# The rotary exchange of groups 4 to 7 moves from transfers into a second matmul, and the steps behind it move forward by one

## The reference

```
x = rmsnorm(tokens) * (1 + 0.1*tanh(scale)) + shift          # scale, shift from cond
q, k, v = split(x @ qkv_w.T + qkv_b)                         # 16 heads of 8 features
q, k = apply_rope(q), apply_rope(k)
#   rope: even' = even*cos - odd*sin ; odd' = even*sin + odd*cos
tokens = tokens + masked_attention(q, k, v) @ out_w.T + out_b      # SELF
query, src = rmsnorm(tokens), rmsnorm(side)
att = masked_attention(query @ wq.T, src @ wk.T, src @ wv.T) @ mha_out_w.T   # CROSS
gate = sigmoid([tokens, update] @ gate_w.T + gate_b); tokens += gate * update
h = rmsnorm(tokens); out = tokens + (silu(h @ g_w.T) * (h @ val_w.T)) @ down_w.T
```

## Time and profile before

| | |
|---|---|
| median of 3 runs | 519.72 us (514.06 to 522.11) |
| profiled execution | 517.94 us, its span 516.1 us |
| PE busy | 442.1 us (86%) |
| DVE busy | 350.1 us (68%) |
| ACT busy | 290.4 us (56%) |
| POOL busy | 190.8 us (37%) |
| mean granted TensorE clock | 0.937 |

### The profile page before, as it was taken

How to read it: one execution, slowest core, us unless ns; L and a number is a source line. 1 busy time by engine, 2 the same in 40 slices (tenths; PEclk the granted TensorE clock), 3 DMA queues, 4 the chain that set the end, 5 groups by cost and what they waited for, 6 DMA issues and landing times.

```text
span 516.1 us, 13226 instructions
## 1 busy us (share of the span) xinstructions
PE 442.1 (86%) x5219; PEld 308.3 (60%) x5219; DVE 350.1 (68%) x655; ACT 290.4 (56%) x644; POOL 190.8 (37%) x184
## 2 busy tenths in 40 slices
PE   3546889878897986999989988999999969999897
PEld 2115375756675664666577655866586748565664
DVE  2326655878885896698677866767748856856565
ACT  4321364577566664777576648486636744556243
POOL 4451140614433163528381828254542542000010
PEclk9975778899997999799999999999989999999999
DMA  3355442354353445344443443425140320000001
GB/s 77 87 174 174 131 122 88 100 162 151 100 162 107 140 121 153 103 128 121 131 137 108 117 140 97 153 67 163 43 149 25 98 92 3 23 3 22 22 1 42
DMA packets 62942, 52.04 MB, mean 101 GB/s; under 512 B 3803, under 2 KB 61728, under 8 KB 62880
## 3 DMA queue, kind: packets, MB, share of 16 engines
q1 hardware_dynamic: 60050, 49.07, 32.2%
q10 hardware_dynamic: 2830, 2.12, 1.4%
HBM read 8.55 MB, written 2.11 MB: 21 GB/s over the span
## 4 chain that ended last, share of the span: by engine, by line
PE 52%; DVE 11%; DMA 10%; ACT 8%; issue 8%; SPq 5%; POOL 4%; ACTq 1%; DVEq 0%; POOLq 0%
PE ps_o L403 8%; PE ps_a L366 7%; PE ps_g L320 7%; PE ps_b L386 6%; PE ps_g L461 5%; SPq L658 4%; DMA k_st<-part_k 4%; DVE top L1087 4%; PE ps_g L444 4%; PE ps_g L353 3%; DMA q_st<-top_t 3%; ACT probs L902 2%; DMA s_in<-in_fside_BxSxS 1%; ACT turned_in L838 1%; PE ps_g L418 1%
## 5 line engine op out<-in xcount | busy, mean ns | idle before, releaser
L1087 DVE TENSOR_REDUCE top<-ps_a 128x4 f32<-128x512 f32 x256 | 169.6, 680 | 106.1 <-PE ps_a L366 104.8
L902 ACT ACTIVATE probs<-ps_b 128x512 f32<-128x512 f32 x256 | 151.3, 595 | 143.6 <-PE ps_b L386 139.5
L366 PE MATMUL ps_a<-k_st,q_st 73*128 73x128 bf16 x1024 | 105.0, 228 | 27.8 <-DMA k_st<-part_k 15.0
L366 PEld LDWEIGHTS ps_a<-k_st,q_st 73*128 73x128 bf16 x1024 | 69.8, 101 | 79.5 <-issue 59.9
L386 PE MATMUL ps_b<-q_st,k_st 75*128 75x128 bf16 x1024 | 102.0, 223 | 9.4 <-ACT probs L902 7.5
L386 PEld LDWEIGHTS ps_b<-q_st,k_st 75*128 75x128 bf16 x1024 | 69.6, 99 | 18.5 <-issue 9.2
L403 PE MATMUL ps_o<-probs,v_pad 128*32 128x128 f32 x2048 | 73.3, 287 | 0.0
L403 PEld LDWEIGHTS ps_o<-probs,v_pad 128*32 128x32 f32 x2048 | 55.3, 115 | 24.1 <-issue 14.7
L728 POOL TENSOR_TENSOR f<-f 128x4 f32<-128x4 f32 x16 | 16.6, 1038 | 98.8 <-DVE f L1136 98.8
L320 PE MATMUL ps_g<-norm,w_t 128*128 128x512 f32 x66 | 37.1, 647 | 1.2 <-DVE hid L1178 1.2
L320 PE MATMUL ps_g<-turned_in,w_t 128*128 128x512 f32 x48 | 30.3, 717 | 5.0 <-ACT turned_in L838 4.8
(11 more groups left out here) (197 smaller groups left out, 677.6 us busy)
## 6 DMA issues: line engine op xcount, KB each, us to landing
q_st<-part_q SPq DMA_DIRECT2D x126, 128.0 KB
k_st<-part_k SPq DMA_DIRECT2D x120, 128.0 KB
x_in<-in_x SPq DMA_DIRECT2D x16, 256.0 KB, 4.5
q_st<-hid SPq DMA_DIRECT2D x18, 128.0 KB
s_in<-in_fside_BxSxS SPq DMA_DIRECT2D x8, 256.0 KB, 5.7
out<-t SPq DMA_DIRECT2D x8, 256.0 KB, 2.3
k_st<-hid SPq DMA_DIRECT2D x12, 128.0 KB
swap_q<-part_q SPq DMA_DIRECT2D x8, 128.0 KB, 2.3
```

The lines of the kernel that those rows point to most:

```text
L366: mm = pe.matmul(ps_a[q % 2][:, j * S:(j + 1) * S], st[0][i][0:R_MAX, h, b * S:(b + 1) * S], st[1][i][0:R_MAX, h, b * S:(b + 1) * S], star ...
L902: act.activation(probs[:, n % 2, q * T:(q + 1) * T], ps_b[q % 2][:, :], ACT.Exp, scale=SCALE).then_inc(exp_done, 1)
L1087: dve.tensor_reduce(top[:, n // 2 % 2, n % 2, QH * q:QH * (q + 1)], ps_a[q % 2][:, :].rearrange("p (h k) -> p h k", h=QH), AX.X, ALU.max). ...
```

## The change

For groups 4 to 7 PE now also makes the exchanged products `qs` and `ks`, as for groups 0 to 3; VectorE multiplies them by the sines into a tile of their own (`sin_q`, and `upd` for k), in the same step as the cosine product; POOL subtracts at +7 and +9. The 16 exchanging transfers go. `upd` is shared with the gate's update, so the sine product of k waits for the last `gate_mul`. For these groups keep_hi, take_hi, keep_mid, take_mid and all stack transfers move one step forward. Order of the pieces: in the step of k's sum POOL has the sum ahead of the side tile's norm, which it had behind it.

```
-        swap_to = [sb("swap_q", [D, T]), upd]
+        sin_q = sb("sin_q", [D, T])
...
         def sined(r, p):
-            if p < 4:
-                return (unit_th, norm3)[r]
-            return part[r][:, 0:2, :].rearrange("d p t -> d (p t)").bitcast(F32)
+            return (unit_th, norm3)[r] if p < 4 else (sin_q, upd)[r]
...  (PE)
-                        if g < 4:
-                            swapped_product(("qs", g), t, 3, W_Q, g)
+                        swapped_product(("qs", g), t, 3, W_Q, g)
                     if t == s_prep(g) + 7:
                         dense(("k", g), t, 3, w_t[:, W_K, :], tokens_tile(g)[:, :])
-                        if g < 4:
-                            swapped_product(("ks", g), t, 3, W_K, g)
+                        swapped_product(("ks", g), t, 3, W_K, g)
...  (SP)
-                    if g >= 4 and t == s_prep(g) + 7:
-                        swap(0, g)
-                    if g >= 4 and t == s_prep(g) + 9:
-                        swap(1, g)
                     for o in range(PARTS):
-                        if t == s_prep(g) + (11, 14, 15)[o]:
+                        if t == s_prep(g) + (11, 14, 15)[o] - (g >= 4):
                             stack(0, o, sp_at)
-                        if t == s_prep(g) + (13, 15, 16)[o]:
+                        if t == s_prep(g) + (13, 15, 16)[o] - (g >= 4):
...  (POOL)
-                else:
-                    pool.wait_ge(swapped[r], 32 * (g - 3))
-                    pool.tensor_tensor(full[r][:, :], full[r][:, :], swap_to[r][:, :], ALU.add
-                                       ).then_inc(summed[r], 1)
...
-                    if t == s_prep(g) + (9 if g >= 4 else 7):
+                    if t == s_prep(g) + 7:
                         rope_sum(0, g)
-                    if t == s_prep(g) + (11 if g >= 4 else 9):
+                    if t == s_prep(g) + 9:
                         rope_sum(1, g)
-                    if t == s_prep(g) + 11:
+                    if t == s_prep(g) + 11 - (g >= 4):
                         take_hi(0, sp_at)
...  (take_hi(1), take_mid(0), take_mid(1): 13, 14, 15, each - (g >= 4); ACT:)
-                    if t == s_prep(g) + 10:
+                    if t == s_prep(g) + 10 - (g >= 4):
                         act.wait_ge(summed[0], g + 1)
                         keep_hi(0, sp_at)
...  (keep_hi(1), keep_mid(0), keep_mid(1): 12, 13, 14, each - (g >= 4); DVE:)
-                if which == 0 and g < 4:
+                if which == 0:
                     key, c = ("qk"[r] + "s", g), C_SWAPPED + r
                     src = full_in(dve, key)
                     wait(dve, summed[r], g)
+                    if r == 1 and g >= 4:
+                        wait(dve, gate_mul, sum(post(e, "residual") < s_prep(g) + 8 for e in range(G)))
...
-                elif which == 0:
-                    parts_free(dve, r, p)
-                    dve.scalar_tensor_tensor(by_batch(sined(r, p)), by_batch(src[:, :]), col[:, c:c + 1], table,
-                                             ALU.add, ALU.mult).then_inc(sin_set[r], 1)
...
-                wait(dve, summed[1], sum(s_prep(e) + 11 < after(g) + 8 for e in range(G)))
+                wait(dve, summed[1], sum(s_prep(e) + 9 < after(g) + 8 for e in range(G)))
...
-                            if t == s_prep(g) + 6 + 2 * r + (which if g >= 4 else 0):
+                            if t == s_prep(g) + 6 + 2 * r:
                                 rope(r, g, which)
```

More of the change, by code:

```diff
@@ L226, in build @@
             sem("x_root"), sem("s_root"), sem("x_normed"), sem("s_normed"))
-        sin_set = [sem("q_sin_set"), sem("k_sin_set")]
-        swapped = [sem("q_swapped"), sem("k_swapped")]
         summed = [sem("q_summed"), sem("k_summed")]
@@ L643, in mask_row @@
                              .unsqueeze(1).to_broadcast([1, H, T])).then_inc(mask_in[p % SETS], 16)
[L645 to L651, removed]
             def stack(r, o, p):
@@ L731, in rope_sum @@
                 taken(pool, ("qk"[r], g))
-                if g < 4:
-                    taken(pool, ("qk"[r] + "s", g))
-                    pool.tensor_tensor(full[r][:, :], full[r][:, :], sined(r, POS[SELF, g])[:, :], ALU.subtract
-                                       ).then_inc(summed[r], 1)
-                else:
-                    pool.wait_ge(swapped[r], 32 * (g - 3))
-                    pool.tensor_tensor(full[r][:, :], full[r][:, :], swap_to[r][:, :], ALU.add
-                                       ).then_inc(summed[r], 1)
+                taken(pool, ("qk"[r] + "s", g))
+                pool.tensor_tensor(full[r][:, :], full[r][:, :], sined(r, POS[SELF, g])[:, :], ALU.subtract
+                                   ).then_inc(summed[r], 1)
             def take_hi(r, p):
@@ L776, in _ @@
                         norm(g, s_in, s_mean, s_ms, s_r, s_root, s_normed)
-                    if t == s_prep(g) + (9 if g >= 4 else 7):
+                    if t == s_prep(g) + 7:
                         rope_sum(0, g)
-                    if t == s_prep(g) + (11 if g >= 4 else 9):
+                    if t == s_prep(g) + 9:
                         rope_sum(1, g)
-                    if t == s_prep(g) + 11:
+                    if t == s_prep(g) + 11 - (g >= 4):
                         take_hi(0, sp_at)
-                    if t == s_prep(g) + 13:
+                    if t == s_prep(g) + 13 - (g >= 4):
                         take_hi(1, sp_at)
-                    if t == s_prep(g) + 14:
+                    if t == s_prep(g) + 14 - (g >= 4):
                         take_mid(0, sp_at)
-                    if t == s_prep(g) + 15:
+                    if t == s_prep(g) + 15 - (g >= 4):
                         take_mid(1, sp_at)
@@ L980, in _ @@
                             keep_xm(g, b)
-                    if t == s_prep(g) + 10:
+                    if t == s_prep(g) + 10 - (g >= 4):
                         act.wait_ge(summed[0], g + 1)
                         keep_hi(0, sp_at)
-                    if t == s_prep(g) + 12:
+                    if t == s_prep(g) + 12 - (g >= 4):
                         act.wait_ge(summed[1], g + 1)
                         keep_hi(1, sp_at)
-                    if t == s_prep(g) + 13:
+                    if t == s_prep(g) + 13 - (g >= 4):
                         keep_mid(0, sp_at)
-                    if t == s_prep(g) + 14:
+                    if t == s_prep(g) + 14 - (g >= 4):
                         keep_mid(1, sp_at)
@@ L1057, in rope @@
                 key, p = ("qk"[r], g), POS[SELF, g]
-                src = full_in(dve, key) if which or g >= 4 else None
                 c = (C_QB, C_KB)[r]
                 table = (sin, cos)[which][:, :].unsqueeze(1).to_broadcast([D, NG, S])
-                if which == 0 and g < 4:
+                if which == 0:
                     key, c = ("qk"[r] + "s", g), C_SWAPPED + r
@@ L1064, in rope @@
                     wait(dve, summed[r], g)
+                    if r == 1 and g >= 4:
+                        wait(dve, gate_mul, sum(post(e, "residual") < s_prep(g) + 8 for e in range(G)))
                     dve.scalar_tensor_tensor(by_batch(sined(r, p)), by_batch(src[:, :]), col[:, c:c + 1], table,
                                              ALU.add, ALU.mult).then_inc(taken_sem(key), 1)
-                elif which == 0:
-                    parts_free(dve, r, p)
-                    dve.scalar_tensor_tensor(by_batch(sined(r, p)), by_batch(src[:, :]), col[:, c:c + 1], table,
-                                             ALU.add, ALU.mult).then_inc(sin_set[r], 1)
                 else:
+                    src = full_in(dve, key)
                     wait(dve, lo_set[r], p)
```

## The result

The changed kernel took 522.82 us (median of 20 runs, 518.19 to 532.30) against 519.18 us for the kernel before (20 runs, 512.96 to 525.45). The ratio is 1.0094, 95% interval 1.0058 to 1.0129: slower by about 5 us, clear of noise and inside 2%. The ratios of this document compare, for each kernel, the runs within 1.5% of its own fastest; the medians of all 20 runs give 1.0070. The forecast was 520.5 us, range 512 to 528, 0.86 for "within 2%". The profiled execution was one of the longer ones (span 526.1 us); so beside it stands a second profile of the same kernel, taken with the last experiments, of 521.0 us. Of the 5.1 us between the two, 3.2 lie in steps 100 to 104 and 1.7 behind step 200, in both places with more time at the slow clock in the longer one.

What follows compares the result with a forecast made beforehand. The prediction took PE (busy 86%) as the bound, except at waits for stacks. Group 4 -2.95, group 5 -3.85, groups 6 and 7 +9.0, split of the tops +0.4: +2.6 on 517.94, so 520.5 us, range 512 to 528.

Steps and rivals of the forecast that it cites:

- PE's price: Groups 4 to 7: two exchanged products cost PE 2.0 us per group, plus 0.3 us waiting for ks's bank.
- The bank wait at steps 113 and 145: Groups 6 and 7: gate unit 4.7 us later, 2.4 of it waiting for the value unit's reader; 4.5 us booked each.
- the sum: Whole kernel: -2.95 - 3.85 + 9.0 + 0.4 = +2.6 us on a profiled 517.94 us, giving 520.5 us.
- Group 4: Stacks gain 3.0 us relative to PE, so the 2.70 us wait goes; -2.95 us with clock and products.
- the prediction's own signs of being wrong: Waits on k_st still over 2 us, PE line 444 without idle, slow clock within the stretches of groups 6 and 7.
- rival 3: Groups 4 and 5: stacks no earlier; 531.9 us if landings move with PE, 527.3 if they stay; chance 0.12.
- Rival 1: Gate-unit waits in groups 6 and 7 cost nothing: 516.1 us, about 514.5 with the slow clock at 140 spared; chance 0.25.
- Group 5: Stacks gain 3.0 us; the 4.39 us wait shrinks to 0.5 and 2.26 us of slow clock goes: -3.85 us.
- With the waits the slow clock goes too: Behind the stack waits of groups 4 and 5 the slow clock vanishes, worth 2.55 and 2.26 us.
- At nothing: Items counted as free: removed transfers, rotary products, `gate_mul` wait, later side norm, a ScalarE wait of 0 to 0.5 us.
- rival 2: PE's clock also falls behind the new gate-unit wait in groups 6 and 7, 2.4 us each: 525.3 us; chance 0.15.
- The port: VectorE's split of the tops slows beside POOL's q sum in groups 4 to 7: up to 2.4 us, 0.4 booked.

Runs made afterwards that it cites:

- experiment 9: The changed kernel with the second gate unit of groups 0 and 1 one step later (steps 114 and 146): 1.0056 of the kernel before.
- experiment 3: The kernel before with only groups 6 and 7 taking the new way, groups 4 and 5 as before: 1.0152 of the kernel before.
- experiment 2: The kernel before with only groups 4 and 5 taking the new way, groups 6 and 7 as before: 1.0035 of the kernel before.
- experiment 4: The changed kernel with the later steps (parts and their stacks) put back; products, sums and banks as changed: 1.0318 of the kernel before.
- experiment 7: The kernel before with the later steps of groups 4 to 7 one step forward, exchange still by transfers, no new products: 1.0162 of the kernel before.
- experiment 12: The kernel before with the residual on GpSimd one step later and nothing else: 0.9962 of the kernel before.
- experiment 5: The changed kernel with the residual on GpSimd (groups 0 to 4) one step later: 1.0105 of the kernel before.
- experiment 8: The kernel before with groups 4 and 5 the new way, 6 and 7 as before, and the GpSimd residual one step later: 0.9959 of the kernel before.
- experiment 10: The changed kernel with the gate units of steps 113 and 145 and the GpSimd residual each one step later: 1.0025 of the kernel before.
- experiment 6: The changed kernel with the exchanged products of groups 4 to 7 made twice into the same bank: 1.0233 of the kernel before.

## Why the prediction was right, and where not

**PE's price: right in kind, a little low.** Forecast 2.0 us per group for two products and 0.3 for ks's bank. The wait of ks was there in each group, 0.51 us at 231.19, from just the reader that the bank bookkeeping named. The four steps in which a group's q and k are made took 2.7 us more at full clock: 8.60 for 5.90 in group 4 (steps 44 to 48), 8.66 for 5.96 in group 6 (108 to 112), and the same in groups 5 and 7. So nothing was hidden, in group 4 either, where the forecast held that possible.

**The bank wait at steps 113 and 145: right in place, cause and size of the whole.** The gate unit was forecast at 4.7 us later than 231.00. It came 4.97 later, with 0.3 of shift from before that place. The wait was 1.79 us against a forecast of 2.4, the products ahead of it took the difference. The timeline of PE and VectorE is the chain that the forecast wrote down, sine and cosine of k ahead of the reader:

```profile
231.19 1.08 PE L327 MATMUL ps_g<-turned_in,w_t 128*64 128x512 f32 x4 [0.51 <-DVE full_q L1047]
231.76 0.75 DVE L1070 TENSOR_SCALAR top_part<-top 128x32 bf16<-128x32 f32 x1
233.26 0.74 DVE L1042 SCALAR_TENSOR_TENSOR upd<-ps_g,col,sin 128x512 f32<-128x512 f32 x1
233.92 0.74 DVE L1047 SCALAR_TENSOR_TENSOR full_k<-ps_g,col,cos 128x512 f32<-128x512 f32 x1
235.18 0.74 DVE L1152 SCALAR_TENSOR_TENSOR hid<-ps_g,late,hid 128x512 f32<-128x512 f32 x1
235.97 1.13 PE L440 MATMUL ps_g<-norm,w_t 128*128 128x512 f32 x2 [1.79 <-DVE hid L1152]
```

The two groups cost 4.3 and 4.1 us against 4.5. They are 2.7 for the four steps with the products and 1.6 and 1.4 for the eight behind them. With the wait gone the trace still shows 3.6 and 3.4 (experiment 9), with it shortened by the order of banks 2.9 (experiment 3). So the wait's own part is 0.7 to 1.4 us per group, less than the 2.2 that the sum had for it. In experiment 9 PE meets the next wait a step or two on, 0.57 us for ScalarE (line 900).

**Group 4: the step failed.** "By the conversion the stacks gain 3.1 us relative to PE, by the queue 3.2; I take 3.0, against a wait of 2.70: gone." It wasn't; a wait over 2 us is one of the prediction's own signs of being wrong. The last start did come earlier, at about 150.4 us (three starts from 149.13, 0.65 apart) instead of 152.48, but from there to the landing it took about 6.1 us instead of 5.16, and PE still waited 2.08 us. The second profile shows 3.19:

```profile
149.13 1.89 SPq L644 DMA_DIRECT2D k_st<-part_k  x3
151.06 0.47 SPq L586 DMA_DIRECT2D s_in<-in_fside_BxSxS  x1
```

```profile
157.52 0.58 PE L362 MATMUL ps_a<-k_st,q_st 73*128 73x128 bf16 x4 [3.19 <-DMA k_st<-part_k]
204.93 0.38 PE L362 MATMUL ps_a<-k_st,q_st 73*128 73x128 bf16 x4 [1.65 <-DMA k_st<-part_k]
```

Of 2.1 us that the starts gained, the landing kept 1.1 (wait ended at 156.79 instead of 157.89). That an earlier start is partly queued in front of the same transfers, the milder form of rival 3, is the likely reason; no run tests it. On the other side PE's products cost their 2.7 us (steps 44 to 48), and the eight steps behind them took 2.8 less (11.51 for 14.31), so that steps 44 to 56 together took 0.1 less than before. In part that is the slow clock at 140 us, which is gone in both profiles. It isn't gone for good: in the profiles of experiments 2 and 4, with the same products, it is there (0.50 and 0.57), and steps 44 to 56 take 21.7 us. Rival 1 had it as a possibility; that PE's busier stretch spares it isn't shown. Nor is the wait a fixed size. In experiment 9, whose edit acts only at step 113, there was no wait for these stacks at all, and steps 44 to 72 took 39.95 us, 2.8 less than before, almost the forecast.

**Group 5: right up to step 100, and given back behind it.** -3.3 and -3.6 us against -3.85: wait of 4.39 gone or 1.65, and full clock in the first steps. But the slow clock didn't go, it came later. In all four profiles in which group 5 is as before (the kernel before, experiments 3, 7 and 12) it lies at steps 95 to 98, and steps 100 to 104 take 5.6 to 5.7 us. In nine of the ten in which group 5 is new it lies at steps 100 to 103, and they take 7.9 to 9.8; the one without it, the second profile, takes 6.5. Steps 72 to 104 together took 49.17 us before and 49.99 and 46.48 in the changed kernel. The forecast's "With the waits the slow clock goes too" is the step that failed here, and it fits experiment 2, where groups 4 and 5 alone brought nothing.

**"At nothing": one item was missing.** The residual on GpSimd ran in the shadow of group 5's stack wait. With the wait gone, its three operations held up the first cross subtraction, and PE stood 2.1 us. But moving the residual took this wait away and not the loss (experiment 5: 9.18 us for steps 100 to 104, experiment 8: 8.10, experiment 10: 7.94), so it explains the wait and not the 4.1 us. What brings the clock down there, with the residual early or late, stays open.

**The clock** fell once more at step 133 in both profiles of the changed kernel (0.50 from 269.5 to 272.5 us in the first), 1.4 us in steps 120 to 140. That isn't rival 2, which had the fall behind the new wait: experiment 8, with groups 6 and 7 as before, has the fall at the same step, and experiment 3, with both groups new, has not. Rival 2 in its own place, behind the wait of the gate unit, came in the profiles of experiments 5 and 6 (in experiment 5 at 1.6 us each and not 2.4), and in neither profile of the changed kernel.

**The port.** The split of the tops took 0.75 us beside q's sum, 0.76 being forecast, and stood in the shadow of PE's later scores. The rule that the prediction takes from the Trainium skill ("SBUF — State Buffer", section "SBUF: two separate sides") agrees with this duration; its full price isn't seen.

The sum came out at +4.9 us in the timed runs and in the second profile, against +2.6. In that profile group 4 was 3.0 us worse than forecast, steps 100 to 104 and 120 to 140 took 0.9 + 1.4 that the sum had at nothing, groups 5 to 7 together came within 0.4, and the rest of the kernel gave 2.2 back. That the total is off by only 2.3 us is in part luck: the stretches of the table alone are off by 4.9, and what gave back had no term in the sum.

## What to carry to other kernels

Where buffers are handed out by a plan in steps, replay the plan with the new requests and look for a buffer whose reader stands in the same step or one before: here that named both new waits to the engine and the line. A plan's numbers only choose who waits, and taking a wait away gives back less than its length (0.7 to 1.4 of 1.8 us here). Before a long wait is taken away, list what the other engines do during it: here work of GpSimd came to hold up PE for 2.1 us. And do not book the slow clock behind a wait as gained with the wait: it came back a few steps later. To find that out, compare the stretch that ends well behind the place, in more than one profile.

## What the runs showed of the hardware

The same transfers land at different times in the same program. For the first scores of position 5 the wait for the stacks was 2.08 and 3.19 us in two profiles of one kernel; with the residual moved, an edit that acts later, it was 0.90; with the gate unit moved, later still, there was none. And the length of a wait doesn't settle whether the clock falls: behind 2.53 us PE went on at full clock (score products of 0.38 us, experiment 4), behind 2.08 us at half (0.58 us):

```profile
156.79 0.58 PE L362 MATMUL ps_a<-k_st,q_st 73*128 73x128 bf16 x4 [2.08 <-DMA k_st<-part_k]
```

Two products of 64 columns each, side by side in one bank, take PE no longer than one of 128 columns: 1.08 us in the timeline for either (L331 in the earlier trace rows, L444 in the earlier trace rows).
